# Attention kernel: the first normalization moved from VectorE to ScalarE, and VectorE's loop end moved by half a pair

## The chip, the cores and the metric

The kernel runs on one core of one Trainium2 chip. The metric is the device time of one execution in microseconds; the kernel before takes 2465.89 us (median of three runs, 2464.13 to 2466.8). Five engines work side by side, each with its own list of instructions, and they meet only at semaphores: TensorE (PE in the profile), VectorE (DVE), ScalarE (ACT), GpSimd (POOL) and SyncE (SP), which here issues the DMAs.

## The reference, cut to what matters

One transformer layer over 64 batches of 128 rows and 512 columns, 16 heads of 32 columns:

```python
emb = silu(_sin_emb(timestep)) @ W_ada + b_ada
scale, shift = split(emb[:, None, :], 2, axis=-1)
x = _ln(src) * (1.0 + scale) + shift          # _ln: (x - mean) / sqrt(var + 1e-5)
q, k, v = x @ Wq + bq, x @ Wk + bk, x @ Wv + bv
scores = einsum('bhqd,bhkd->bhqk', q / sqrt(32), k) + attention_bias
probs = softmax(where(src_mask, -inf, scores))
x = x + (einsum('bhqk,bhkd->bhqd', probs, v) @ Wo + bo)
h = _ln(x) * g2 + beta2
ff = _gelu2(h @ W1 + b1) @ W2 + b2            # x * sigmoid(1.702 x)
return x + ff
```

The change touches only the first `_ln`, that of `src`.

## The kernel before, in words

Three parts follow each other: a short setup (the gains and offsets of the layer, the weights split in a high and a low piece), the attention (to about 1110 us of the profile) and the feed-forward part. Products are made from three matmuls each, high times high, high times low and low times high.

The attention works on 32 pairs of batches. A step is half a pair: step (p, 0) attends to batch t = 2p, step (p, 1) to batch t = 2p + 1, and in the same step the engines prepare later batches: step (p, 0) makes the keys and step (p, 1) the queries of pair p + 1, both make values, both turn (transpose) a batch of pair p + 2, and the statistics and the normalization run ahead of that by up to one pair more. The 16 heads of a batch go in four groups. The order on each engine is written out by hand. `run` (L579) unrolls the steps of pairs -2 to 3 and 28 to 32, and puts pairs 4 to 27 in a loop of six iterations of four pairs, eight steps each. VectorE has its own frame, `run_halves` (L897): it cuts a step in `first_half` and `second_half` and places the end of its loop (L904) between the two halves of an even step, (p, 0).

The names that matter below:

- `normalize` (L117) makes xn = (xin - mean) * rstd for one batch, on VectorE, as the last thing of `first_half` of every step: the second batch of pair p + 2 in step (p, 0), the first batch of pair p + 3 in step (p, 1).
- `statistics` and `spread` (L102, L107), in step (p, 0) only, right after it: mean and variance of pair p + 3. They write over `mean`, so `spread` first waits until both batches of pair p + 2 are normalized: `xn_ready` must have reached 2(p + 3). The seven small instructions of the variance are in `variance` (L48); POOL makes rstd of it in `root` (L113).
- `residual` (L122): POOL multiplies xn by the gains and adds the offsets (L127, L129). PE turns the result (L135), ACT copies it as xT_hi (L140), DVE makes xT_lo (L145).
- `second_half` begins with `context` (L68, L70): DVE splits psC, the product of the probabilities and the values (PE L962), into cT_hi and cT_lo, from which PE makes the output projection (psD<-wo, L923 to L925). Then come the reciprocals of the softmax sums (`invert`, L791, a group each), which POOL waits for (L597), and xT_lo.
- `first_half` begins with the four score additions (L780), then `add_bv` (L772, the values), the maxima (L785), `negate_mask` (L796), and `add_residual` (L806, L808), which frees psD[0].
- PE: `project_t` makes keys or queries in four pieces, a = 0 to 3. Piece 0 waits for `add_bv` of the same step, and piece 1 for L806 of the same step.
- ACT: `copy_k` and `copy_q` (L698, L702) copy the four pieces out of psD, `exps` (L713) makes the exponentials of a group, `copy_pT` (L708) copies turned probabilities, `norm.high` is L140.
- SP: `norm.load` (L94) fetches xin of pair p + 4 in step (p, 0), once `xn_ready` has reached 2(p + 3); `load_gains` (L98) stands behind it.

Of the kernel before, what the change touches and what calls it, by code (L numbers as in the profile page):

```python
# [25 lines left out]
ALU = mybir.AluOpType  # L26
# [14 lines left out]
def at_least(eng, sem, count):  # L41

    if isinstance(count, int) and count <= 0:
        return
    eng.wait_ge(sem, count)
# [27 lines left out]
class FirstNorm:  # L73

    def __init__(self, nc, ctx, hold, x, ident, psX):
        sb = lambda name, shape, dt=F32: ctx.enter_context(nc.sbuf_tensor(name, shape, dt))
        sem = lambda name: hold.enter_context(nc.semaphore(name))
        B, _, DM = x.shape
        self.DM, self.CH, self.ident, self.psX = DM, DM // P, ident, psX
        self.rows = x.rearrange("b s n -> s b n")  # L80
        self.xin, self.xn = sb("xin", [P, 2, 2, DM]), sb("xn", [P, 2, DM])
        self.xres, self.adab = sb("xres", [P, 4, 2, DM]), sb("adab", [P, 2, 2 * DM])
        self.st, self.part = sb("st", [P, 2, 6]), sb("part", [P, 4, 2])
        self.mean, self.ve, self.rstd, self.expo = sb("mean", [P, 2]), sb("ve", [P, 2]), sb("rstd", [P, 2]), sb("expo", [P, 2])
        self.xT = [[sb(f"xT{u}_{n}", [P, self.CH, 2 * P], F32R) for n in ("hi", "lo")] for u in range(2)]
        self.x_in = [sem(f"x_in{u}") for u in range(2)]
        self.bn_done, self.part_done, self.var_ready, self.rstd_ready, self.xn_ready = (
            sem("bn_done"), sem("part_done"), sem("var_ready"), sem("rstd_ready"), sem("xn_ready"))
        self.adab_in = [sem(f"adab_in{b}") for b in range(2)]
        self.res_half, self.res_ready = sem("res_half"), sem("res_ready")  # L90
        self.xt_done, self.x_hi, self.x_split = sem("xt_done"), sem("x_hi"), sem("x_split")
        self.w_low = {n: sem(f"w{n}_low") for n in "vkq"}
# [21 lines left out]
        at_least(pool, self.var_ready, q + 1)  # L114
        pool.tensor_tensor(self.rstd[:, :], self.ve[:, :], self.expo[:, :], ALU.pow).then_inc(self.rstd_ready, 1)

    def normalize(self, dve, q, u, b):  # L117
        at_least(dve, self.rstd_ready, q + 1)
        at_least(dve, self.res_half, q * 2 + (b - 1))
        dve.tensor_scalar(self.xn[:, b, :], self.xin[:, u, b, :], self.mean[:, b:b + 1], self.rstd[:, b:b + 1],  # L120
                          ALU.subtract, ALU.mult).then_inc(self.xn_ready, 1)

    def residual(self, pool, q, slot, b):
        out = self.xres[:, slot, b, :]
# [208 lines left out]
def setup_part(nc, block, hold, d, w, norm, ada_rows, bq_s, bk_c, bv_bc, raw_o, wo_in, bo_bc):  # L333
# [6 lines left out]
    with ExitStack() as ctx:  # L340
# [85 lines left out]
        @block.scalar  # L426
        def _(act):
            def high(i):
                act.wait_ge(w_in[i], DMA)
                if names[i] == "v":  # L430
                    act.activation(split_w[i][0][:, :, :], raw[i][:, :, :], ACT.Copy).then_inc(w_hi, 1)
                    return
                for c in range(CH):
                    last = act.activation(in_slots(split_w[i][0], c), by_slot(raw[i], c), ACT.Copy)
                last.then_inc(w_hi, 1)

            act.wait_ge(rest_ok, 1)
            act.activation(emb[:, :], rest[:, :], ACT.Sin).then_inc(sin_ok, 1)
            act.wait_ge(sin_ok, 1)
            act.activation(expm[:, :], emb[:, :], ACT.Exp, scale=-1.0).then_inc(exp_ok, 1)  # L440
            for i in range(3):
                high(i)

# [16 lines left out]
        @block.vector  # L460
        def _(dve):
            count = [0]

            def then(ins):
                count[0] += 1
                ins.then_inc(chain, 1)
                dve.wait_ge(chain, count[0])


            dve.wait_ge(small_in, 3 * DMA)  # L470
            then(dve.tensor_copy(col[:, 0:1], t_int[:, :]))
            then(dve.tensor_scalar(col[:, 1:2], col[:, 0:1], 1.0 / NUM_STEPS, None, ALU.mult))
            then(dve.tensor_copy(q_hi[:, :], col[:, 1:2]))
            then(dve.tensor_tensor(col[:, 2:3], col[:, 1:2], q_hi[:, :].bitcast(F32), ALU.subtract))
            then(dve.scalar_tensor_tensor(out=col[:, 3:4], in0=q_hi[:, :].bitcast(F32), scalar=-NUM_STEPS,
                                          in1=col[:, 0:1], op0=ALU.mult, op1=ALU.add))
            then(dve.scalar_tensor_tensor(out=col[:, 4:5], in0=col[:, 2:3], scalar=-NUM_STEPS,
                                          in1=col[:, 3:4], op0=ALU.mult, op1=ALU.add))
            then(dve.scalar_tensor_tensor(out=col[:, 5:6], in0=col[:, 4:5], scalar=1.0 / NUM_STEPS,
                                          in1=col[:, 1:2], op0=ALU.mult, op1=ALU.add))  # L480
            then(dve.tensor_scalar(col[:, 6:7], col[:, 5:6], RESCALE, None, ALU.mult))
            then(dve.tensor_scalar(angle[:, :], freqs[:, :], col[:, 6:7], None, ALU.mult))

            k, r = turns[:, :], rest[:, :]
            dve.wait_ge(quarter_ok, 5)
            then(dve.tensor_scalar(k, angle[:, :], 1.0 / TWO_PI, quarter[:, 0:1], ALU.mult, ALU.add))
            then(dve.tensor_scalar(k, k, ROUND, None, ALU.add))
            then(dve.tensor_scalar(k, k, ROUND, None, ALU.subtract))
            then(dve.scalar_tensor_tensor(out=r, in0=k, scalar=-PI_A, in1=angle[:, :], op0=ALU.mult, op1=ALU.add))
            then(dve.scalar_tensor_tensor(out=r, in0=k, scalar=-PI_B, in1=r, op0=ALU.mult, op1=ALU.add))  # L490
            then(dve.scalar_tensor_tensor(out=r, in0=k, scalar=-PI_C, in1=r, op0=ALU.mult, op1=ALU.add))
            then(dve.tensor_scalar(r, r, quarter[:, 1:2], None, ALU.add))
            dve.tensor_scalar(r, r, 3.1415925, -3.1415925, ALU.min, ALU.max).then_inc(rest_ok, 1)
            norm.statistics(dve, 0, 0)
            norm.spread(dve, 0)

            dve.wait_ge(exp_ok, 1)
            then(dve.tensor_scalar(expm[:, :], expm[:, :], 1.0, None, ALU.add))
            then(dve.reciprocal(expm[:, :], expm[:, :]))
            dve.tensor_tensor(gate[:, :], emb[:, :], expm[:, :], ALU.mult).then_inc(gate_ok, 1)  # L500
            norm.normalize(dve, 0, 0, 0)
            dve.wait_ge(gate_turned, 1)
            dve.tensor_copy(embT[:, :, :, :], psT[:, :, :].rearrange("p c (a b) -> p a c b", a=2)).then_inc(embT_ok, 1)
            dve.wait_ge(bias_in, 11 * DMA)
            dve.tensor_scalar(bq_s[:, :], bq_raw[:, :], HD ** -0.5, None, ALU.mult)
            low(dve, 0, range(CH))

            dve.wait_ge(ada_done, 1)
            dve.scalar_tensor_tensor(out=ada[:, 0:DM], in0=psA[:, 0, :], scalar=1.0, in1=b_ada[:, 0:DM],
                                     op0=ALU.add, op1=ALU.add).then_inc(ada_ok, 1)  # L510
            dve.wait_ge(ada_done, 2)
            dve.tensor_tensor(ada[:, DM:], psA[:, 1, :], b_ada[:, DM:], ALU.add).then_inc(ada_ok, 1)
            low(dve, 1, range(CH))
            low(dve, 2, range(CH // 2))
# [21 lines left out]
def attention_part(nc, block, hold, d, w, norm, ada_rows, resid, psD, bq_s, bk_c, bv_bc, bo_bc, raw_o, wo_in, second, weights):  # L536
# [7 lines left out]
    with ExitStack() as ctx:  # L544
# [149 lines left out]
        def _(act):  # L694
# [22 lines left out]
            def step(p, u, b, on):  # L717
# [26 lines left out]
                    exps(t, b, 1)  # L744
                if on.proj:
                    copy(*kq, 3)
                if on.turn:
                    norm.high(act, p + 2, u % 2, b)
                if on.attn:
# [18 lines left out]
        def _(dve):  # L768
# [41 lines left out]
            def first_half(p, u, b, on):  # L810
# [22 lines left out]
                else:  # L833
# [15 lines left out]
                    if on.attn:  # L849
                        for g in range(2, G):  # L850
                            highest(t, b, g)
                if on.norm:
                    if b:
                        norm.normalize(dve, p + 3, (u + 3) % 2, 0)
                    else:
                        norm.normalize(dve, p + 2, u % 2, 1)
                if on.stats:
                    norm.statistics(dve, p + 3, (u + 3) % 2)
                if on.attn:
                    invert(t, b, 0)  # L860
                if on.stats:
                    norm.spread(dve, p + 3)

            def second_half(p, u, b, on):
                t = p * 2 + b
                if on.prev:
                    context(t - 1)
                if on.attn:
# [27 lines left out]
            def run_halves():  # L896

                first, last = 4, PAIRS - 5
                for p in range(-2, first):
                    for b in range(2):  # L900
                        first_half(p, p % UNROLL, b, half(p, b, PAIRS))
                        second_half(p, p % UNROLL, b, half(p, b, PAIRS))
                first_half(first, first % UNROLL, 0, steady(0))
                with dve.Fori(0, (last - first + 1) // UNROLL) as i:  # L904
                    for m in range(2 * UNROLL):
                        u, b = divmod(m, 2)
                        second_half(i * UNROLL + (first + u), (first + u) % UNROLL, b, steady(b))
                        u, b = divmod(m + 1, 2)
                        first_half(i * UNROLL + (first + u), (first + u) % UNROLL, b, steady(b))
                for p in range(last + 1, PAIRS + 1):  # L910
                    for b in range(2):
                        if p > last + 1 or b:
                            first_half(p, p % UNROLL, b, half(p, b, PAIRS))
                        second_half(p, p % UNROLL, b, half(p, b, PAIRS))

            run_halves()

# [795 lines left out]
```

## Time and profile before

| | |
|---|---|
| median of three runs | 2465.89 us (2464.13 to 2466.8) |
| the profiled execution, its time | 2472.93 us |
| its span, first to last instruction | 2471.1 us |
| its mean granted TensorE clock | 0.988 |
| PE busy, matmuls | 2363.4 us, 96% |
| DVE busy | 1830.4 us, 74% |
| POOL busy | 1840.8 us, 74% |
| ACT busy | 1323.4 us, 54% |

The page gives busy time over the whole span. The attention and the feed-forward part have different limits, so the busy shares say little about a change in one of them; the timeline of each engine in one pair of steps, the idle time in square brackets with what ended it, and the chain of waits around VectorE's loop end say more. Times in rows are in us from the start of the span.

### The profile page before, as it was taken

How to read it: one execution, taken by the hardware profiler on the slowest of the kernel's cores; microseconds unless marked ns; L12 is line 12 of the kernel's file. 1: busy time of each engine (PE TensorE's matmuls, PEld its weight loads, DVE VectorE, ACT ScalarE, POOL GpSimd, SP SyncE). 2: the span in 40 equal slices, each digit the busy share in tenths (PEclk: the TensorE clock that was granted, in tenths of full speed). 3: DMA queues.
4: the chain of work that ended last, by engine and by line, in shares of the span. 5: the costliest groups of instructions: out<-in, count | busy, mean ns of one | idle time of the engine just before them, and what ended most of it. 6: DMA issues, size and time to landing. Idle time of an engine off the chain costs nothing.

```text
span 2471.1 us, 61234 instructions
## 1 busy us (share of the span) xinstructions
PE 2363.4 (96%) x21010; PEld 2234.2 (90%) x21010; DVE 1830.4 (74%) x2921; ACT 1323.4 (54%) x3663; POOL 1840.8 (74%) x1785
## 2 busy tenths in 40 slices
PE   4999999999999999987999999999989999999998
PEld 3888888888888888867999999999979999999998
DVE  4788888888888888777666666666577676777776
ACT  2566666566666666575555555555543333343332
POOL 3777777777777777778777777777896777767675
PEclk8999999999999999999999999999999999999999
DMA  7344444344434444333343434343465556555563
GB/s 241 109 134 134 139 140 134 110 134 139 139 115 137 135 139 136 102 90 122 147 159 136 161 144 154 141 161 146 159 219 170 185 181 188 184 183 187 170 196 125
DMA packets 288978, 372.26 MB, mean 151 GB/s; under 512 B 28544, under 2 KB 202752, under 8 KB 288768
## 3 DMA queue, kind: packets, MB, share of 16 engines
q1 hardware_dynamic: 288768, 369.57, 46.2%
q8 instruction: 118, 1.93, 0.3%
q14 instruction: 92, 0.75, 0.1%
HBM read 251.81 MB, written 117.70 MB: 150 GB/s over the span
## 4 chain that ended last, share of the span: by engine, by line
PE 85%; DVE 5%; issue 3%; POOL 3%; ACT 1%; DMA 1%; SPq 0%; DVEq 0%; POOLq 0%; ACTq 0%
PE up L1568 14%; PE up L1566 14%; PE up L1567 14%; PE turn L923 5%; PE psD L923 4%; PE psD L924 4%; PE psD L925 4%; PE turn L925 4%; PE turn L924 4%; PE psS L952 4%; PE psC L962 2%; PE psS L938 2%; PE turn L1566 2%; PE turn L1567 2%; PE turn L1568 2%
## 5 line engine op out<-in xcount | busy, mean ns | idle before, releaser
L1566 PE MATMUL up<-T,wc 128*128 128x256 f32 x1792 | 511.2, 285 | 14.7 <-DVE gu L1440 7.0
L1568 PE MATMUL up<-T,wc 128*128 128x256 f32 x1792 | 508.0, 283 | 0.0
L1567 PE MATMUL up<-T,wc 128*128 128x256 f32 x1792 | 505.4, 282 | 0.0
L597 POOL TENSOR_TENSOR s<-s,rinv 128x512 f32<-128x512 f32 x254 | 265.2, 1045 | 234.2 <-DVE rinv L791 231.7
L713 ACT ACTIVATE s<-s,nmx 128x128 f32<-128x128 f32 x1024 | 396.2, 394 | 5.5 <-issue 5.5
L1566 PE MATMUL up<-wc,gs 128*128 128x256 f32 x1280 | 360.2, 281 | 3.2 <-DVE gs L1523 3.2
L657 POOL TENSOR_TENSOR bias<-bias,mneg 128x512 f32<-128x512 f32 x256 | 351.8, 1394 | 13.7 <-DVE mneg L796 13.7
L1567 PE MATMUL up<-wc,gs 128*128 128x256 f32 x1280 | 359.9, 281 | 0.0
L1568 PE MATMUL up<-wc,gs 128*128 128x256 f32 x1280 | 359.8, 281 | 0.0
L1566 PEld LDWEIGHTS up<-T,wc 128*128 128x128 f32 x1792 | 339.3, 189 | 18.5 <-DVE gu L1440 8.4
L1567 PEld LDWEIGHTS up<-T,wc 128*128 128x128 f32 x1792 | 340.7, 190 | 0.0
L1568 PEld LDWEIGHTS up<-T,wc 128*128 128x128 f32 x1792 | 337.2, 188 | 0.0
L1523 DVE TENSOR_TENSOR gs<-gbuf,gs 128x768 fp32r<-128x768 f32 (+1 forms) x128 | 197.0, 1565 | 104.2 <-ACT gs L1399 104.2
L1523 DVE TENSOR_TENSOR gs<-gu,gs 128x768 fp32r<-128x768 f32 x126 | 198.5, 1608 | 81.2 <-ACT gs L1399 81.2
L1566 PEld LDWEIGHTS up<-wc,gs 128*128 128x128 f32 x1280 | 241.9, 189 | 3.8 <-DVE gs L1523 3.8
L1567 PEld LDWEIGHTS up<-wc,gs 128*128 128x128 f32 x1280 | 241.9, 189 | 0.0
L1568 PEld LDWEIGHTS up<-wc,gs 128*128 128x128 f32 x1280 | 241.9, 189 | 0.0
L1399 ACT ACTIVATE gs<-gbuf 128x768 fp32r<-128x768 f32 (+1 forms) x128 | 115.2, 945 | 198.8 <-PE up L1568 189.0
L1399 ACT ACTIVATE gs<-gu 128x768 fp32r<-128x768 f32 x126 | 113.5, 946 | 185.9 <-PE up L1568 176.7
L1246 POOL TENSOR_TENSOR gu<-gu,p5c 128x256 f32<-128x256 f32 x128 | 101.7, 794 | 131.5 <-ACT p5c L1340 110.3
L713 ACT ACTIVATION_READ_ACCUMULATOR s<-s,nmx 128x1 f32 x1024 | 197.8, 193 | 0.0
L785 DVE TENSOR_REDUCE nmx<-s 128x4 f32<-128x512 f32 x256 | 167.3, 674 | 0.1
(209 smaller groups left out, 7043.8 us busy)
## 6 DMA issues: line engine op xcount, KB each, us to landing
bias<-in_bias SPq DMA_DIRECT2D x128, 512.0 KB, 5.4
gated<-gu SPq DMA_DIRECT2D x128, 512.0 KB, 2.6
adab<-ada_rows SPq DMA_DIRECT2D x64, 512.0 KB, 5.5
gbuf<-gated SPq DMA_DIRECT2D x64, 512.0 KB, 3.9
gu<-gated SPq DMA_DIRECT2D x63, 512.0 KB, 3.9
xin<-in_x SPq DMA_DIRECT2D x32, 512.0 KB, 5.1
resid<-rout SPq DMA_DIRECT2D x64, 256.0 KB, 2.2
r<-resid SPq DMA_DIRECT2D x16, 1024.0 KB, 6.0
```

Of the source, the lines that this page charges most:

```text
L597: eng.tensor_tensor(s[:, b, heads, :], s[:, b, heads, :], rinv[:, b, heads].unsqueeze(2).to_broadcast([P, HG, S]), ALU.mult).then_inc(done, 1)
L657: pool.tensor_tensor(bias[:, b, heads, :], bias[:, b, heads, :], mneg[:, b, :].unsqueeze(1).to_broadcast([P, HG, S]), ALU.add).then_inc(bi ...
L713: last = act.activation(s[:, b, h, :], s[:, b, h, :], ACT.Exp, bias=nmx[:, b, h:h + 1], accum_out=sums[:, b, h:h + 1])
L785: dve.tensor_reduce(nmx[:, b, heads], s[:, b, heads, :], mybir.AxisListType.X, ALU.max, negate=True).then_inc(nmax_ready, 1)
L923: pe.matmul(out, sh, mh, start=start, stop=False)
L924: pe.matmul(out, sh, ml, start=False, stop=False)
L925: return pe.matmul(out, sl, mh, start=False, stop=stop)
L1399: act.activation(gs[s % 2][:, 0, ops, :], t[:, ops.start + 1:ops.stop + 1, :], ACT.Copy).then_inc(s_hi, 1)
L1523: dve.tensor_tensor(gs[s % 2][:, 1, ops, :], t[:, ops.start + 1:ops.stop + 1, :], gs[s % 2][:, 0, ops, :].bitcast(F32), ALU.subtract).then ...
L1566: pe.matmul(out_ap, sh, mh, start=start, stop=False)
L1567: pe.matmul(out_ap, sh, ml, start=False, stop=False)
L1568: return pe.matmul(out_ap, sl, mh, start=False, stop=stop)
```

## The change

`normalize` goes from VectorE to ScalarE. There it is one activation, rstd * xin + offset, and a new small instruction on VectorE, `center`, makes offset = -mean * rstd for both batches of a pair. ScalarE normalizes in each step behind the copy of the fourth piece of the keys or queries and ahead of xT_hi; `center` stands at the start of `second_half` of odd steps, (p, 1). `statistics`, `invert` of group 0 and `spread` move from the end of `first_half` to the start of `second_half`, which leaves their place in VectorE's order as it was. The wait in `spread` is unchanged. VectorE's loop end, which stays between the halves, is now in the odd step, behind the maxima of a pair's second batch. In the setup the first batch's normalization goes behind ScalarE's exponential.

```diff
@@ FirstNorm
+        self.offset, self.offset_ready = sb("offset", [P, 2]), sem("offset_ready")
...
-    def normalize(self, dve, q, u, b):
+    def center(self, dve, q):
+
         at_least(dve, self.rstd_ready, q + 1)
-        at_least(dve, self.res_half, q * 2 + (b - 1))
-        dve.tensor_scalar(self.xn[:, b, :], self.xin[:, u, b, :], self.mean[:, b:b + 1], self.rstd[:, b:b + 1],
-                          ALU.subtract, ALU.mult).then_inc(self.xn_ready, 1)
+        dve.scalar_tensor_tensor(out=self.offset[:, :], in0=self.mean[:, :], scalar=-1.0, in1=self.rstd[:, :],
+                                 op0=ALU.mult, op1=ALU.mult).then_inc(self.offset_ready, 1)
+
+    def normalize(self, act, q, u, b):
+        at_least(act, self.offset_ready, q + 1)
+        at_least(act, self.res_half, q * 2 + (b - 1))
+        act.activation(self.xn[:, b, :], self.xin[:, u, b, :], ACT.Identity, scale=self.rstd[:, b:b + 1],
+                       bias=self.offset[:, b:b + 1]).then_inc(self.xn_ready, 1)
@@ setup, scalar
+            norm.normalize(act, 0, 0, 0)
@@ setup, vector
-            norm.normalize(dve, 0, 0, 0)
+            norm.center(dve, 0)
@@ attention, scalar step
                 if on.proj:
                     copy(*kq, 3)
+                if on.norm:
+                    if b:
+                        norm.normalize(act, p + 3, (u + 3) % 2, 0)
+                    else:
+                        norm.normalize(act, p + 2, u % 2, 1)
                 if on.turn:
                     norm.high(act, p + 2, u % 2, b)
@@ attention, vector
-                if on.norm:
-                    if b:
-                        norm.normalize(dve, p + 3, (u + 3) % 2, 0)
-                    else:
-                        norm.normalize(dve, p + 2, u % 2, 1)
+
+            def second_half(p, u, b, on):
+                t = p * 2 + b
+                if on.norm and b:
+                    norm.center(dve, p + 3)
                 if on.stats:
                     norm.statistics(dve, p + 3, (u + 3) % 2)
                 if on.attn:
                     invert(t, b, 0)
                 if on.stats:
                     norm.spread(dve, p + 3)
-
-            def second_half(p, u, b, on):
-                t = p * 2 + b
@@ run_halves
                 first_half(first, first % UNROLL, 0, steady(0))
+                second_half(first, first % UNROLL, 0, steady(0))
+                first_half(first, first % UNROLL, 1, steady(1))
                 with dve.Fori(0, (last - first + 1) // UNROLL) as i:
-                    for m in range(2 * UNROLL):
+                    for m in range(1, 2 * UNROLL + 1):
```

## Rows read from the trace of the kernel before

**Rows 1.** The page, busy us (share of the span) and instructions: TensorE.
```profile
PE 2363.4 (96%) x21010; PEld 2234.2 (90%) x21010; DVE 1830.4 (74%) x2921; ACT 1323.4 (54%) x3663; POOL 1840.8 (74%) x1785
```
**Rows 2.** Timeline of PE, line 938: start us, us, engine line op names xcount.
```profile
205.69 1.06 PE L938 MATMUL psS<-kf,qf 32*128 32x128 f32 x28
...
431.04 1.17 PE L938 MATMUL psS<-kf,qf 32*128 32x128 f32 x32
446.88 1.17 PE L938 MATMUL psS<-kf,qf 32*128 32x128 f32 x32
...
984.80 0.95 PE L938 MATMUL psS<-kf,qf 32*128 32x128 f32 x24
```
**Rows 3.** Chain of waits around VectorE's loop end: start us, us, what.
```profile
462.83 4.89 issue
...
594.04 3.91 issue
```
**Rows 4.** Timeline of PE; brackets: idle before it, and what ended it.
```profile
437.81 0.28 PE L923 MATMUL turn<-xT_hi,wq_hi 128*128 128x256 f32 x1
439.99 0.36 PE L923 MATMUL psD<-xT_hi,wq_hi 128*128 128x256 f32 x1
...
469.49 0.47 PE L923 MATMUL psD<-wo_hi,cT_hi 128*128 128x512 f32 x1 [2.64 <-DVE cT_lo L70]
473.11 0.38 PE L923 MATMUL turn<-xT_hi,wq_hi 128*128 128x256 f32 x1 [0.58 <-DVE v L772]
476.15 0.39 PE L923 MATMUL psD<-xT_hi,wq_hi 128*128 128x256 f32 x1 [0.52 <-DVE rout L806]
```
**Rows 5.** Timeline of DVE in one undisturbed pair.
```profile
428.25 0.16 DVE L53 TENSOR_TENSOR part<-st 128x2 f32<-128x2 f32 x1
...
431.05 0.69 DVE L68 CAST cT_hi<-psC 128x512 fp32r<-128x512 f32 x1
432.38 0.17 DVE L791 RECIPROCAL rinv<-sums 128x4 f32<-128x4 f32 x1
...
441.88 1.56 DVE L120 TENSOR_SCALAR xn<-xin,mean,rstd 128x512 f32<-128x512 f32 x1
...
446.43 0.69 DVE L68 CAST cT_hi<-psC 128x512 fp32r<-128x512 f32 x1 [2.90 <-PE psC L962]
```
**Rows 6.** Timeline of DVE behind the loop end of rows 3.
```profile
469.26 0.17 DVE L791 RECIPROCAL rinv<-sums 128x4 f32<-128x4 f32 x1
...
473.65 1.26 DVE L796 TENSOR_SCALAR mneg<-mask 128x128 f32<-128x128 uint8 x1
```
**Rows 7.** Timeline of POOL at the same time.
```profile
473.54 1.29 POOL L129 TENSOR_TENSOR xres<-xres,adab 128x512 f32<-128x512 f32 x1
```
**Rows 8.** Timeline of ACT in the even step of rows 5.
```profile
426.50 0.46 ACT L698 ACTIVATE kf<-psD,bk_c 128x256 f32<-128x256 f32 x1
426.86 1.08 ACT L708 ACTIVATE pT<-psS 128x512 f32<-128x512 f32 x2
...
430.05 0.46 ACT L698 ACTIVATE kf<-psD,bk_c 128x256 f32<-128x256 f32 x1
431.14 0.60 ACT L140 ACTIVATE xT_hi<-turn 128x512 fp32r<-128x512 f32 x1 [0.64 <-PE turn L135]
```
**Rows 9.** Groups by form, ACT: out<-in shapes xcount, busy us, mean ns of one, idle before.
```profile
L708 ACT ACTIVATE pT<-psS 128x512 f32<-128x512 f32 x256 | 138.5, 595 | 11.8 <-PE psS L952 11.8
L255 ACT ACTIVATE hTf<-turn,be_c,g_c 128x256 f32<-128x256 f32 x120 | 59.1, 562 | 0.0
L1335 ACT ACTIVATE p1c<-up 128x256 f32<-128x256 f32 x128 | 49.0, 383 | 151.3 <-PE up L1568 135.0 <-DVE gu L1435 15.4
```
**Rows 10.** Timeline of DVE in an early step, POOL idle beside it.
```profile
38.28 0.16 DVE L53 TENSOR_TENSOR part<-st 128x2 f32<-128x2 f32 x1
...
39.17 0.69 DVE L145 TENSOR_TENSOR xT_lo<-turn,xT_hi 128x512 fp32r<-128x512 f32 x1
```
**Rows 11.** Timeline of PE, step (0, 1).
```profile
85.61 0.38 PE L923 MATMUL turn<-xT_hi,wq_hi 128*128 128x256 f32 x1 [1.82 <-DVE v L772]
```

More of the change, by code:

```diff
@@ L911, in run_halves @@
                     for b in range(2):
+                        if p > last + 1:
+                            first_half(p, p % UNROLL, b, half(p, b, PAIRS))
                         if p > last + 1 or b:
-                            first_half(p, p % UNROLL, b, half(p, b, PAIRS))
-                        second_half(p, p % UNROLL, b, half(p, b, PAIRS))
+                            second_half(p, p % UNROLL, b, half(p, b, PAIRS))
             run_halves()
```

## The prediction

> **What bounds the kernel now.** I read the page first: PE is busy 96% of the span [rows 1]. Only the attention is touched, so the next view is PE's timeline there. The score matmuls, L938, come once a step; in an undisturbed stretch they stand 15.84 us apart [rows 2], and PE has no idle time that a wait ended. PE sets the pace, and work taken off DVE or put on ACT is worth nothing by itself. From 205.69 to 984.80 us lie 48 steps, the six iterations of the loop [rows 2]: 779.11 us, where 48 x 15.84 = 760.32. So 18.8 us are lost, and the same view between the two ends shows where: five iterations are 3.4 to 4.5 us longer than eight steps, and the first is not. The chain of waits puts that at VectorE's loop end, L904. DVE's sequencer takes the jump back and issues nothing for 4.89 us at worst and 3.91 us at best, five times [rows 3]. The jump stands just ahead of `context`, in an even step in which DVE has no idle time; so cT_lo comes late (2.64 us of PE idle in the worst iteration), then the values (0.58) and then the rout addition L806 (0.52) [rows 4]. These three waits with the reordering around them are the 18.8 us. The chain, the idle time in brackets and PE's timeline agree, so this sum I take as the most that the moved loop end can give.
>
> **The moved loop end.** Five jumps remain, and I leave their price at 3.9 to 4.9 us [rows 3]. In an odd step DVE is through with the maxima at 441.88, where the normalization stood, and then waits for PE until 446.43 [rows 5]. With the normalization gone the cover is 446.43 - 441.88 = 4.55 us, less 0.2 for one reciprocal, and `center`, a small instruction (0.16 to 0.2 like its neighbours, up to some 1.3 if POOL is in its way). At 4.9 plus 0.4 `context` would be up to 0.8 late. What is late next is cT_lo, and the worst jump shows its slack: of its 4.89 us only 2.64 were left as idle time of PE [rows 3, 4], so `context` can be some 2.2 late for nothing. The jump is therefore hidden: -18.8 us, bounds 0 (not hidden at all) and -18.8. The Trainium skill, "Runtime: NRT & Kernel Launch", section "Instruction fetch mechanics", says that a taken branch whose target lies outside the two pages held forces a fetch; this row agrees with it for DVE, and by it the stall goes along with the branch, it only gets another cover.
>
> **The normalization on DVE** is removed 64 times, 1.56 us each [rows 5]; for the reason above that gives PE nothing in steady steps. In the even step it only makes DVE idle earlier. The DMAs that SP issues behind the same semaphore (xin, then the gains) go out some 4 us later in the even step; they are needed a pair later, about 30 us, and SP's next store is not due before the next step: nothing.
>
> **The normalization on ACT** is an activation of 512 columns with two operands from SBUF. With two such operands and 256 columns it takes 562 ns; 256 more columns cost 595 - 383 = 212 ns [rows 9]; together 0.775 us, and 0.80 with a little for the SBUF source, which no row with this form shows (bounds 0.70 and 0.90). In the order of ACT it falls into the idle 0.64 us ahead of xT_hi [rows 8], so that xT_hi is 0 to 0.1 late, with slack behind it. ACT pays nothing in steady steps.
>
> **The wait that this turns on.** `spread` in the even step waits until the second batch of pair p + 2 is normalized. Before, DVE had just done that itself. Now it is done on ACT behind the fourth copy of the keys, and DVE waits there with everything behind `spread`: `context`, two reciprocals for which POOL waits, xT_lo, and the whole next `first_half`. Step by step, in the times of the undisturbed pair:
> - The fourth copy starts at 430.05, and the next activation starts 0.36 later, as at 426.50 and 426.86 [rows 8]: 430.41. It ends at 430.41 + 0.80 = 431.21.
> - `spread` has two more waits to pass: some 0.2 (an estimate with the bounds 0.05 and 0.35, since no row shows this form; the nearest are two instructions with a wait between them, 0.1 to 0.2 apart). L53 starts at 431.42.
> - The seven small instructions take 2.80 us before [rows 5], as two of them stood in POOL's way; POOL is idle at the new place, because its group 0 comes earlier (the reciprocal is no longer behind the normalization) and its next work waits for the next reciprocal. The undisturbed price is 39.17 - 38.28 = 0.89 [rows 10]. `context` starts at 432.31 instead of 431.05 [rows 5], 1.26 late.
> - The reciprocal of group 1, which frees POOL, goes from 432.38 to 433.64. From here the disturbed iteration is the pattern, because there too nothing is waited for behind it: from this reciprocal to PE's first query matmul is 473.11 - 469.26 = 3.85, and to PE's piece 1 is 476.15 - 469.26 = 6.89 [rows 4, 6]. So PE could start piece 0 at 437.49, before its 437.81: nothing lost. But piece 1 can start at 440.53 only, and stood at 439.99 [rows 4]: 0.54 us late.
> - The 6.89 hold because L796 starts 0.11 behind POOL's L129 and lasts until it is through [rows 6, 7]; both follow from the same reciprocal, so they keep this distance.
>
> The Trainium skill, "SBUF — State Buffer", section "Who interferes with whom", says the one of VectorE and GpSimd that issues first holds the shared port for its whole instruction and the other fully blocks, and that ACT never waits. The 1.26 us of L796 agree. By the rule taken alone the change is all gain, as ACT would do undisturbed what DVE did blocked; the row of the wait speaks against it.
>
> All pairs with statistics and an L806 in the odd step pay this, p = 1 to 28: 28 x 0.54 = 15.1 us. The bounds for one pair are 0 (the slack of 1.26 - 0.54 = 0.72 not used up) and 0.54 + 0.3.
>
> **The head.** In steps (-1, 1) and (0, 0) ACT has no gap ahead of xT_hi and PE later waits for `add_bv`, twice, as in step (0, 1) [rows 11]; the activation pushes both by its slot of 0.7: 1.4 us (bounds 0 and 3). The setup is covered by the wait for the weights.
>
> **The sum.** -18.8 + 15.1 + 1.4 = -2.3 us. Against the profiled execution's own 2472.93 this is 2470.6; against the median, 2465.89, it is 2463.6. I take the sum over to the median unscaled, since the pairs lie in a stretch at full clock. About 0.2%, 4.9 us, is what a measurement can tell from no change.
>
> **The rivals.**
> - A, the forecast: jump hidden, 0.54 a pair; 0.40 to 0.68 a pair gives 2459.7 to 2467.5. Chance 0.58.
> - B, the wait in `spread` is covered: the activation ends earlier, or L796 issues just ahead of L129 (it is 0.11 away) and L806 comes up to 1.2 earlier. Then -18.8 + 1.4 = -17.4: 2448.5. For it: 0.72 us of slack, the thin distance. Against it: five disturbed iterations, all alike. Chance 0.21.
> - C, slower: `spread` at its new place meets POOL. If one of its instructions waits for a POOL instruction as before (2.80 instead of 0.89, of which one half is about 0.9), a pair loses 1.4 us: -17.4 + 28 x 1.4 = +22, 2488. It decides above 0.80 a pair, where the sum passes +4.9. Against it: POOL waits for the reciprocal that DVE has not yet made. Chance 0.11.
> - D, the change doesn't do what it says: the jump in the odd step is not covered, for example because it now starts with the bias loads that go out behind L808. Without any cover -2.3 + 18.8 = +16.5: 2482; covered by half, 2473. Chance 0.10.
>
> **The numbers.** Faster by over 0.2%: B whole and some 0.15 of A's lower end, 0.36. Slower: C, most of D, 0.19. Within: 0.45. The time is A's, 2463.6. The range goes from 2447, 1.5 below B, to D with half a cover, 2473, which leaves out C, the worse half of D and the edges of B.
>
> **What would show it.** Right: L938 at 31.68 + 0.54 a pair, no longer iteration among them; PE idle ahead of psD<-xT_hi,wq_hi, ended by rout L806, some 0.5 us in each odd step; DVE idle ahead of L53, ended by ACT's xn; the jump's 4 us inside idle time that PE's psC ends. Wrong: L53 with no ACT wait (B), L55 or L57 at 1 us (C), cT_lo ending PE's idle in the step behind the jump (D).

## The result, and the profile after

The changed kernel takes 2476.75 us (median of 20; 2469.77 to 2479.66) beside 2467.94 for the kernel before on the same chip (20; 2463.08 to 2475.41): a ratio of 1.0027 [1.0017, 1.0036]. By the ratio that is slower by 6.7 us (4.2 to 8.9), where 2.3 us less had been forecast; 2476.75 lies above the range. The medians differ by 8.8, since the executions of both kernels fall in two groups some 8 us apart (of which more below), and more of the changed kernel's fall in the upper one. One execution of the change measured again (r4 below) took 5178.39 us; no profile shows why, the ratio given there leaves it out, and the median of ten does not. The profiled execution took 2478.87 us with a span of 2477.1; the kernel before had 2471.1. So its span is 6.0 longer, and this is what the profiles can explain. The page, as [rows 1]:

```profile
PE 2376.5 (96%) x21010; PEld 2241.7 (90%) x21010; DVE 1695.0 (68%) x2889; ACT 1365.0 (55%) x3727; POOL 1841.1 (74%) x1785
```

DVE lost 135 us of work, ACT took on 42, and PE, which sets the pace, got busier by 13 with the same instructions. The timeline of PE, the score matmuls that open a step (start, duration), as [rows 2]:

```profile
405.73 1.17 PE L951 MATMUL psS<-kf,qf 32*128 32x128 f32 x32
...
438.01 1.17 PE L951 MATMUL psS<-kf,qf 32*128 32x128 f32 x32
```

A pair takes 32.28 where 31.68 stood before. Between the two lies the start 422.09: 16.36 for the odd step, 15.92 for the even one. DVE and ACT in this pair, as [rows 5, 8]:

```profile
405.09 0.81 ACT L127 ACTIVATE xn<-xin,offset,rstd 128x512 f32<-128x512 f32 x1
```
```profile
406.02 0.16 DVE L53 TENSOR_TENSOR part<-st 128x2 f32<-128x2 f32 x1 [4.52 <-ACT xn L127]
...
406.91 0.69 DVE L68 CAST cT_hi<-psC 128x512 fp32r<-128x512 f32 x1
...
408.24 0.17 DVE L804 RECIPROCAL rinv<-sums 128x4 f32<-128x4 f32 x1
...
412.63 1.28 DVE L809 TENSOR_SCALAR mneg<-mask 128x128 f32<-128x128 uint8 x1
...
414.43 0.68 DVE L819 TENSOR_TENSOR rout<-psD,xres 128x512 f32<-128x512 f32 x1
```

PE's two pieces behind the reciprocal at 408.24, and PE's waits from 200 to 1000 us (total, times, longest), as [rows 4]:

```profile
412.53 0.28 PE L936 MATMUL turn<-xT_hi,wq_hi 128*128 128x256 f32 x1
...
415.16 0.39 PE L936 MATMUL psD<-xT_hi,wq_hi 128*128 128x256 f32 x1 [0.17 <-DVE rout L819]
```
```profile
PE psD L936 <- DVE rout L819: 5.9, 24, 0.5
```

This is the wait of the forecast: DVE idle until ACT's xn, then rout late, then PE idle ahead of piece 1. From reciprocal to piece 1 it is 6.92, 6.89 had been taken over from the disturbed iteration [rows 4, 6]. Piece 0 comes on time. The idle time of 0.17 is smaller than the loss of the step, because PE's order around the wait spreads it: the matmuls psS<-ident,s, up to the start of what follows them and so with that idle time, take 3.58 us in this pair and 3.17 in a pair before.

The loop end, in DVE's timeline and in the rows of its sequencer (form, ns, start), as [rows 3]:

```profile
L916 DVEq COMPARE_BRANCH  x1: 63/63/63, 350.9 to 350.9; - x1
L916 DVEq FUSED_REGOPS  x1: 70/70/70, 353.9 to 353.9; - x1
```
```profile
353.97 0.52 DVE L121 SCALAR_TENSOR_TENSOR offset<-mean,rstd 128x2 f32<-128x2 f32 x1 [0.70 <-issue]
354.41 0.17 DVE L804 RECIPROCAL rinv<-sums 128x4 f32<-128x4 f32 x1
357.10 0.69 DVE L68 CAST cT_hi<-psC 128x512 fp32r<-128x512 f32 x1 [2.52 <-PE psC L975]
```

The jump takes 3.0 us of the sequencer (2.8 to 3.1 in the five of this profile; 4.0 to 5.0 by the same rows before), and most of that passes while DVE still works off what had been issued; 0.70 are left as idle time. Behind it DVE waits 2.52 us for PE: the jump is hidden.

### The profile page after: what moved, and what is told of

It is laid out like the page before. It is cut to its first block, busy times and chain, and to the rows that moved or that the text cites. A ratio compares the mean times of both kernels' runs of the same rounds, so it can differ in the third digit from the quotient of the medians.

```text
span 2477.1 us, 61290 instructions
## 1 busy us (share of the span) xinstructions
PE 2376.5 (96%) x21010; PEld 2241.7 (90%) x21010; DVE 1695.0 (68%) x2889; ACT 1365.0 (55%) x3727; POOL 1841.1 (74%) x1785
## 4 chain that ended last, share of the span: by engine, by line
PE 75%; DVE 12%; issue 5%; ACT 5%; POOL 3%; DMA 1%; DVEq 0%; SPq 0%; ACTq 0%; POOLq 0%
PE up L1581 13%; PE up L1579 13%; PE up L1580 13%; PE psD L936 3%; PE turn L936 3%; PE psS L965 3%; PE turn L938 3%; PE turn L937 3%; PE psD L937 3%; PE psD L938 3%; PE turn L1579 2%; PE turn L1581 2%; PE turn L1580 2%; DVE s L793 2%; ACT s L721 2%
```

## The experiments

All of them compute the whole reference. The tables give medians in us. The kernel before, run beside them, had 2467.53 (e1 to e4), 2469.98 (e5 to e8), 2470.34 (r1 to r4) and 2471.38 (s1 to s4). "Even, odd" are the two steps of an undisturbed pair in the profile.

**Each part alone.** E2 is the kernel before with the loop end moved and DVE normalizing as it did; E3 is the changed kernel with the loop end back in the even step.

```diff
 # e2, against the kernel before (e3 the other way round, against the changed one)
+            def second_half(p, u, b, on):
+                t = p * 2 + b
                 if on.norm:
...
+                second_half(first, first % UNROLL, 0, steady(0))
+                first_half(first, first % UNROLL, 1, steady(1))
                 with dve.Fori(0, (last - first + 1) // UNROLL) as i:
-                    for m in range(2 * UNROLL):
+                    for m in range(1, 2 * UNROLL + 1):
```

> The kernel before with only VectorE's loop end moved into the odd step, behind the maxima; normalization stays on VectorE. Theory (the jump is hidden in the idle time that ends with psC): the five iterations with a jump lose nothing or up to 0.5 us each where they lost 3.4 to 4.5, a time 15 to 19 us below the kernel before. Rival (the jump stalls wherever it stands, and the changed kernel only pays for it elsewhere): within 5 us of the kernel before.

> The kernel with the loop end alone once more, since its first measurement had four runs. If the loop end is worth the five stalls and nothing else, the time is 15 to 19 us below the kernel before; the first measurement had 20. Its step of 15.75 us comes again if it belongs to the program, and is 15.84 or 15.92 if it belongs to the execution.

> The changed kernel with VectorE's loop end back in the even step, so the normalization's move alone. Theory (in the even step VectorE now idles some 4.5 us ahead of L53 for ScalarE's normalization, and the jump of 3 to 5 us falls into that): the five jumps cost at most 0.5 us each more, so the time is within 3 us of the changed kernel, and a pair takes 32.27. Rival (only the moved loop end hides the jump): some 17 us above the changed kernel, 24 above the kernel before.

| kernel | median (n) | ratio to before | even, odd | step at an iteration's end |
|---|---|---|---|---|
| before, again (r1) | 2470.22 (10) | 1.0004 [0.9988, 1.0019] | 15.84, 15.84 | 19.5 to 20.1 |
| loop end alone (e2) | 2447.95 (4) | 0.9916 [0.9888, 0.9944] | 15.75, 15.75 | 15.75 |
| the same again (r2) | 2448.16 (6) | 0.9917 [0.9899, 0.9934] | 15.84, 15.84 | 15.84 |
| ACT normalizes, loop end as before (e3) | 2473.47 (10) | 1.0020 [1.0007, 1.0034] | 15.92, 16.35 | 16.37 |
| the change again (r4) | 2471.70 (10) | 1.0012 [0.9995, 1.0029] | 15.92, 16.35 | 16.71 |

> The kernel before, unchanged, as one more profile of it. It tells whether the 15.84 us of an undisturbed step belong to the program or to the execution: if to the program (its addresses), 15.84 again; if to the execution or the chip, another value, such as 15.92 or 15.75, and then the 0.08 us a step are not the change's.

> The changed kernel, unchanged, on the same chip. By the causes found so far: 15.92 in even steps and 16.3 to 16.4 in odd ones if both belong to the program, 3 to 10 us above the kernel before, and 20 to 27 above the loop end alone.

R1 is the kernel before unchanged; the first profile of it had 19.2 to 20.4 in the last column. R4 is the change unchanged: its steps came as expected, its time only 0.12% above the kernel before, with an interval that holds no change. So the 6.7 us rest on the first measurement, and r4 does not contradict them. R2, the timelines of PE over the second jump and of DVE at the first:

```profile
441.38 1.17 PE L941 MATMUL psS<-kf,qf 32*128 32x128 f32 x32
...
473.06 1.17 PE L941 MATMUL psS<-kf,qf 32*128 32x128 f32 x32
```
```profile
342.08 0.57 DVE L120 TENSOR_SCALAR xn<-xin,mean,rstd 128x512 f32<-128x512 f32 x1 [0.92 <-issue]
...
345.89 0.69 DVE L68 CAST cT_hi<-psC 128x512 fp32r<-128x512 f32 x1 [3.15 <-PE psC L965]
```

The loop end alone is worth 17 to 21 us by the ratios of e2, r2 and s3 (s3, below, has one unused semaphore more), which fits the 18.8 of the forecast. That it is more is not shown: the 56 steps behind the head lose 18.3 us in r2 against the first profile of before and 19.9 against r1. It doesn't need the normalization's place on DVE: the normalization behind the jump takes 0.57 here instead of 1.56 (0.55 to 0.86 behind the five jumps; POOL is nearly through by then), and 3.15 us of cover are left. E3 shows the other half: with the normalization on ACT the stalls are gone although the loop end stands where it stood. DVE is idle there for ACT's xn anyway, and the jump, 2.8 to 3.0 us in e3, lies in that idle time. The two parts thus remove the same 18.8 us, and together not twice; what the normalization costs beside that is left over in both e3 and the change.

**The wait in `spread`.** E1 lets `spread` wait for DVE's own offset and moves the wait for ACT's xn to POOL's `root`; e4 leaves the wait and runs ACT's activation ahead of the first copy of the even step.

```diff
 # e1
     def spread(self, dve, q):
-        at_least(dve, self.xn_ready, q * 2)
+        at_least(dve, self.offset_ready, q)
     def root(self, pool, q):
+        at_least(pool, self.xn_ready, q * 2)
 # e4
+                if on.norm and not b:
+                    norm.normalize(act, p + 2, u % 2, 1)
                 if on.proj:
...
-                if on.norm:
-                    if b:
-                        norm.normalize(act, p + 3, (u + 3) % 2, 0)
-                    else:
-                        norm.normalize(act, p + 2, u % 2, 1)
+                if on.norm and b:
+                    norm.normalize(act, p + 3, (u + 3) % 2, 0)
```

> The changed kernel, but spread no longer waits for the normalized batches; POOL's root does, which stands two POOL instructions later, and spread waits only for the center of the pair before. Theory (the wait of spread for ScalarE's normalization costs 0.5 to 0.6 us a pair): PE no longer waits for the rout addition in odd steps, a pair takes 31.7 us again instead of 32.27, and the time falls by some 16 us against the changed kernel, to about 15 to 18 us below the kernel before if the head costs little. Rival (the activation's slot on ScalarE is what costs): a pair stays at 32.2 or more and the time is that of the changed kernel, 5 to 9 us above the kernel before.

> The changed kernel with the even step's normalization on ScalarE moved ahead of the first copy of the keys, into the 4.6 us in which ScalarE waits for PE; the wait in spread stays. Theory: the semaphore is there long before spread asks, a pair takes 31.7 us, PE has no wait for rout, and the time is that of the kernel with the wait moved to root within 3 us, 15 to 18 us below the kernel before. Rival (the wait is not the cause): the time of the changed kernel.

E1 2464.59 (10), 0.9981 [0.9965, 0.9996]; e4 2461.03 (10), 0.9966 [0.9947, 0.9984]. Both have 15.92 in even and odd steps alike and no step of the 56 above 16.1, and PE waits for nothing between 200 and 970 us. E1, the timelines of DVE and of PE (its odd step):

```profile
397.10 0.16 DVE L53 TENSOR_TENSOR part<-st 128x2 f32<-128x2 f32 x1
...
400.88 0.69 DVE L68 CAST cT_hi<-psC 128x512 fp32r<-128x512 f32 x1 [0.90 <-PE psC L976]
```
```profile
401.33 1.17 PE L952 MATMUL psS<-kf,qf 32*128 32x128 f32 x32
...
417.25 1.17 PE L952 MATMUL psS<-kf,qf 32*128 32x128 f32 x32
```

L53 has no wait for ACT, and `context` waits for PE again. Two edits with nothing in common but the wait both take the odd step's excess away, so the wait is its cause. Both expectations of the time missed: 15 to 18 us below the kernel before were expected, and by the ratios it was 4.7 and 8.4. The profiles show where most of that went: the 56 steps take 14.0 and 14.3 us less than before, some 4.5 short of 18.8 for a reason that the next runs look for, and the two steps of the head take 3.3 and 1.1 more. The rest lies behind the attention, where executions differ by more than that.

**The 0.08 us in every step.** Even steps are 15.92 in the changed kernel, where nothing waits, and e1 and e4 keep that. The new tensor `offset` moves every later one up by 32 bytes (xT_hi from 136512 to 136544). E5 is the kernel before with the unused tensor and semaphore, r3 is e2 with them, s3 e2 with the semaphore alone, s4 e2 with the tensor alone. S1 is the changed kernel, and s2 is e4, with the offset in two spare columns of `mean`, so that nothing moves. E6, e7 and e8 are the changed kernel, e1 and e4 with `offset` widened to 64 bytes.

```diff
 # e5, r3 (s3: the semaphore alone, s4: the tensor alone)
+        self.offset, self.offset_ready = sb("offset", [P, 2]), sem("offset_ready")
 # e6, e7, e8
-        self.offset, self.offset_ready = sb("offset", [P, 2]), sem("offset_ready")
+        self.offset, self.offset_ready = sb("offset", [P, 16]), sem("offset_ready")
 # s1, s2
-        self.mean, ... = sb("mean", [P, 2]), ...
+        self.mean, ... = sb("mean", [P, 4]), ...
-        dve.scalar_tensor_tensor(out=self.offset[:, :], in0=self.mean[:, :], ...
+        dve.scalar_tensor_tensor(out=self.mean[:, 2:4], in0=self.mean[:, 0:2], ...
```

> The kernel before with nothing but the unused tensor offset (and its unused semaphore) allocated where the changed kernel allocates it; every tensor behind it, from xT to rout, lies 32 bytes higher in each partition, and no instruction is different otherwise. Theory (the 32 bytes take PE's operands off a 64-byte boundary, and PE is slower by them without any wait): an undisturbed step takes 15.92 us as in the changed kernel, not 15.84, so some 60 steps cost 5 us. Rival (the 0.08 us come from ScalarE or VectorE working beside PE, or from the execution): a step of 15.75 to 15.84 and the time of the kernel before.

> The changed kernel with offset padded to 64 bytes a partition, so that the tensors behind it lie on 64-byte boundaries again; the instructions are the same. Theory (alignment): even steps take 15.84 us or less instead of 15.92, odd ones 16.2 to 16.3 as the wait for rout stays, and the time is 4 to 9 us below the changed kernel, within 3 us of the kernel before. Rival: as the changed kernel.

> The kernel with the wait moved from spread to root, with offset padded to 64 bytes. Theory (loop end, wait and alignment are the three causes and add up): no wait of PE in the loop and steps of 15.75 to 15.84 us, 4 to 9 us below the same kernel without the padding, so 10 to 15 us below the kernel before and some 5 us above the kernel with the loop end alone, which is what the head keeps. Rival (the padding does nothing): 2 to 5 us below the kernel before.

> The kernel with the even step's normalization ahead of the first copy of the keys, with offset padded to 64 bytes. Theory: steps of 15.75 to 15.84 us, no wait in the loop, 12 to 20 us below the kernel before, near the kernel with the loop end alone. Rival (the padding does nothing): 6 to 8 us below the kernel before.

> The loop end alone, with the unused tensor offset in the place where the changed kernel has it. If PE's step depends on the addresses behind it, a step takes 15.92 us and the time is 5 to 10 us above the loop end alone; if it depends on the execution, the two times are equal within 3 us.

> The loop end alone, with one unused semaphore more and no tensor. If the addresses make the step longer: 15.84 us a step and the time of the loop end alone, 20 us below the kernel before. If the semaphore does: 15.92 and 12 below.

> The loop end alone, with the unused tensor and no semaphore. If the addresses make the step longer: 15.92 us a step and 11 to 13 us below the kernel before. If the semaphore does: 15.84 and 20 below.

> The changed kernel with offset in the unused half of the mean tile, so that nothing behind it moves; the instructions are the same. If the addresses make the step longer: even steps 15.84, odd ones 16.25 to 16.3, a time 5 to 9 us below the changed kernel and 0 to 4 below the kernel before, which is where the forecast had it. If the semaphore does: as the changed kernel.

> The kernel with the even step's normalization ahead of the first copy of the keys, with offset in the mean tile. If the addresses make the step longer: 15.84 us in all steps and 5 to 9 us below the shifted one, so 14 to 19 us below the kernel before. If the semaphore does: 15.92 and 8 to 10 below.

| kernel | moved by | median (n) | ratio to before | even, odd |
|---|---|---|---|---|
| e5, before | 32 B | 2474.31 (12) | 1.0019 [1.0006, 1.0032] | 15.92, 15.92 |
| e6, change | 64 B | 2472.30 (12) | 1.0015 [1.0001, 1.0030] | 15.92, 16.37 |
| e7, e1 | 64 B | 2460.28 (11) | 0.9969 [0.9952, 0.9986] | 15.92, 15.92 |
| e8, e4 | 64 B | 2460.79 (12) | 0.9959 [0.9945, 0.9972] | 15.92, 15.92 |
| r3, e2 | 32 B | 2456.98 (6) | 0.9951 [0.9937, 0.9966] | 15.92, 15.92 |
| s3, e2 | 0 | 2451.32 (4) | 0.9931 [0.9906, 0.9957] | 15.84, 15.84 |
| s4, e2 | 32 B | 2450.50 (4) | 0.9920 [0.9897, 0.9943] | 15.92, 15.92 |
| s1, change | 0 | 2473.81 (10) | 1.0002 [0.9990, 1.0015] | 15.84, 16.33 |
| s2, e4 | 0 | 2457.41 (5) | 0.9943 [0.9922, 0.9964] | 15.84, 15.84 |

In the profiles this has no exception: of eleven with the tensor at the new addresses all have 15.92, and of seven without none has it: five have 15.84, e2 has 15.75, and s2 has 15.75 up to 319 us and 15.84 behind it, for which I have no reason. The semaphore does nothing. Where the time goes is seen in the matmuls themselves, with nothing waiting. PE's timeline, first and tenth matmul of the same piece, first r2 (not moved), then r3:

```profile
448.16 0.28 PE L926 MATMUL turn<-xT_hi,wk_hi 128*128 128x256 f32 x1
...
449.19 0.28 PE L926 MATMUL turn<-xT_hi,wk_hi 128*128 128x256 f32 x1
```
```profile
451.54 0.28 PE L927 MATMUL turn<-xT_hi,wk_hi 128*128 128x256 f32 x1
...
452.60 0.28 PE L927 MATMUL turn<-xT_hi,wk_hi 128*128 128x256 f32 x1
```

Nine distances take 1.03 us in r2 and 1.06 in r3: 0.114 and 0.118 each. My reason for it fell: I took it that xT_hi had lost a 64-byte boundary, but in e6 to e8 its address is a multiple of 64 again (136576) and the steps stay at 15.92. PE's timeline narrows it. In a pair without a jump, the products that read xT (values, keys and queries) take 17.51 us in r1, r2 and s3, 17.66 in r3, s4, e5 and e4, and 17.68 in e7 and e8; all other matmuls of the pair take 14.16 to 14.18 in every one of them, though cT, kf, qf, pT and v moved as well. So the excess is in the products with xT, and no 64-byte boundary is the rule; what the rule is, is open.

Addresses are not all that sets this pace. In the feed-forward part wc and gs lie at the same addresses in all these kernels, and yet their matmuls follow each other in 0.117, 0.119 or 0.120 us, one value for an execution from some 1900 us to the end, at full granted clock and with nothing waiting. PE from 2050 to 2350 us (length, busy, matmuls, granted clock, DMA share, GB/s), e2 and then r2, which are the same kernel:

```profile
2050.00:2350.00 300.00, 300.00 (x2503) 1.00 0.59 185
```
```profile
2050.00:2350.00 300.00, 300.00 (x2559) 1.00 0.60 186
```

The change had 0.119 in its first profile and 0.117 in r4. From one value to the next the time behind the attention grows by some 6.5 us, which is most of the distance of the two groups of executions. No run tells what chooses the value.

In the times the effect of the address is at the edge. Sixty steps of 0.08 are 4.8 us. R3 is 8.8 above r2 and e5 0.19% above before, s2's ratio lies 0.0023 below e4's and s1's 0.0010 and 0.0025 below those of the change; but s4 and s3, with four executions each, differ the other way. The rest of the kernel differs from execution to execution by more than this: of the kernel before, some lie around 2464 and some around 2472. So several expectations of the time missed though the steps came: s4 is 21 us below before and not 11 to 13, s1 2.4 above it and not 0 to 4 below, and e7 and e8 lie 9.7 and 9.2 below, where their rivals, the padding doing nothing, had at most 5 and 8.

## Why the prediction was wrong

The profiled executions differ by 6.0 us, and this divides as follows. Up to the first of these steps (64.71 against 64.43) 0.3; the two steps of the head 34.60 against 30.38, that is 4.2; the 56 steps behind them 905.78 against 905.83, that is 0; what follows 1472.0 against 1470.5, that is 1.5.

**The moved loop end: right.** -18.8 us was taken, and r2 shows it: no step from the third to 980 us is longer than 16.10. The estimated cover of 4.55 us less 0.4 was not even needed in full, since the jump cost 2.8 to 3.1 at its new place. It doesn't cost a fixed time, and the place alone doesn't set it: e3 has the loop end at the old place and jumps in 2.8 to 3.0. The long ones, 4.0 to 5.0, are in the three profiles (before, r1, e5) in which DVE normalizes and the loop end stands in the even step; why is open. What the forecast missed is that the normalization on ACT hides the jump by itself (e3). That changes no term of the sum, but it turns the credit round: the loop end needs no normalization on ACT to be worth 18.8.

**The wait in `spread`: right in every link, size nearly right.** The activation was to start 0.63 ahead of the score matmuls (measured 405.09 against 405.73, 0.64), to take 0.80 (0.81), `spread` to start 0.38 behind them (0.29), its seven instructions to take 0.89 (0.89), and piece 1 to be 0.54 late. The odd step is longer than the even one by 0.43 in the change and by 0.49 in s1, where nothing else is added. In s1 24 pairs at 0.49 and four at 0.37 to 0.41 are 13.3 us, where 28 x 0.54 = 15.1 stood. In the change the same sum is 11.6, because its even steps have grown by 0.08 and its odd ones by 0.02 only: the wait takes up a part of the slower matmuls. Rival B, a covered wait, and rival C, `spread` in POOL's way, did not come.

**A late start that I did not have: +2.1 us.** The six steps at an iteration's end are 16.70, 0.35 longer than the other odd ones. It is not the jump itself. The timelines of ACT, DVE and PE in the first of them:

```profile
340.22 0.80 ACT L127 ACTIVATE xn<-xin,offset,rstd 128x512 f32<-128x512 f32 x1
```
```profile
341.50 0.16 DVE L53 TENSOR_TENSOR part<-st 128x2 f32<-128x2 f32 x1 [4.88 <-ACT xn L127]
```
```profile
350.63 0.39 PE L936 MATMUL psD<-xT_hi,wq_hi 128*128 128x256 f32 x1 [0.50 <-DVE rout L819]
```

L53 starts 0.48 behind the end of xn, where it starts 0.12 behind it in the pair shown above. PE is late at 350.63, before the jump at 350.9, and it comes a sixth time, with L53 at 989.05, where no jump back follows. E6, r4 and s1 have the same six. In e3, with the loop end elsewhere, it is 0.12 to 0.14 in all 24 pairs of the loop, and no step is longer. In the pairs ahead of the loop, whose code is unrolled, it is 0.03, and these are the four with the smaller loss. So it goes with where the waiting instruction stands in the loop's code; by what means I can't say. With all this the steps come to -18.8 + 11.6 + 2.1 + 56 x 0.08 = -0.6, and some 0.5 lie in three steps that are 0.14 to 0.20 longer: -0.1, as measured.

**The addresses: +2.8 us in these steps, missing from the sum.** This is the term that the forecast did not have at all. The edit "add a tensor" was costed at nothing, without being named. What it cost is the difference of two kernels that differ in nothing else: the 56 steps take 905.8 us in the change and 903.0 in s1, so without it they would have gained 2.9 us on the kernel before and not nothing. In kernels where PE waits for nothing in these steps it costs the full 56 x 0.08 = 4.5 (r3 takes 4.2 more than r2).

**The head: mechanism right, size wrong.** The two waits for `add_bv` came as forecast (start, duration, idle before), beside 3.44 and 1.82 before:

```profile
73.20 0.58 PE L936 MATMUL turn<-xT_hi,wk_hi 128*128 128x256 f32 x1 [4.34 <-DVE v L785]
...
88.53 0.39 PE L936 MATMUL turn<-xT_hi,wq_hi 128*128 128x256 f32 x1 [2.42 <-DVE v L785]
```

They are 1.5 longer together, for 1.4 forecast. The other 2.7 are TensorE's clock. The table by stretches (busy of PE, PEld, DVE, ACT, POOL, then the granted clock, DMA share, GB/s), of the changed kernel and then of the kernel before:

```profile
70.00:80.00 10.00, 6.80 (x37) 6.80 (x38) 7.02 (x14) 2.48 (x10) 5.29 (x5) 0.66 0.41 108
80.00:90.00 10.00, 7.58 (x70) 6.40 (x69) 6.21 (x19) 6.64 (x28) 6.25 (x7) 0.94 0.35 117
90.00:100.00 10.00, 10.00 (x118) 9.50 (x121) 3.25 (x7) 8.11 (x27) 6.71 (x6) 0.88 0.51 150
```
```profile
70.00:80.00 10.00, 7.98 (x63) 7.81 (x66) 9.53 (x20) 4.41 (x20) 6.26 (x5) 0.83 0.70 207
80.00:90.00 10.00, 8.18 (x82) 7.21 (x75) 7.36 (x15) 6.57 (x28) 8.94 (x9) 1.00 0.39 111
90.00:100.00 10.00, 10.00 (x115) 8.64 (x113) 5.14 (x11) 7.76 (x32) 7.15 (x8) 1.00 0.17 57
```

A granted clock of 0.66 in ten microseconds is 6.8 us at 1.2 GHz instead of 2.4; with the 0.94 and the 0.88 it is 10.4 in all, where the kernel before has 3.4 from its 0.83. Seven microseconds more at half the clock can cost up to 3.5, and 2.7 is what has to be explained. No run was made for it, but the kept profiles settle it, since e2 and r2 are one kernel, with the same two waits (5.3 and 5.2 us). The two steps of the head in e2 and then in r2, columns as above:

```profile
64.33:97.31 32.98, 27.71 (x241) 25.09 (x241) 21.50 (x40) 17.54 (x63) 20.26 (x18) 0.84 0.39 114
```
```profile
63.83:92.64 28.81, 23.57 (x241) 20.96 (x241) 21.86 (x40) 17.27 (x63) 19.99 (x18) 1.00 0.45 130
```

At 0.84 the same work takes 4.2 us more than at full clock. The kernel before has 0.94 and 30.38 us, the change 0.85 and 34.60: e2's 32.98 with the waits 1.5 longer. What the activation's slot has to do with the clock is less clear. In all seven profiles of kernels with this activation in its slot behind the fourth copy the second of the two steps is 17.34 to 17.42, and the head takes 33.7 to 34.7; in six of the eight with DVE normalizing the second step is 15.1, in e2 and s4 16.73, and the head takes 28.8 to 33.0. E4 and e8, with the activation moved forward, have 15.12 and 15.14, but s2 has 16.72. So the slot goes with the longer step each time, and the other kernels have it now and then too. The forecast's bound of 3 for the head, set without the clock, was too low.

**What follows, 1.5 us,** lies in a part that the change doesn't touch, and differs by more than that between executions of one kernel (1472.0 and 1465.5 in the change, 1477.3 and 1461.7 in e2 and r2). I take it for no effect, but that is not shown: 6.7 us by the ratio are some 2 more than the 4.5 that the profiles have up to there.

**The baseline, 2.1 us,** belongs to neither kernel: the forecast's 2463.6 started from a median of three executions, 2465.89, where twenty gave 2467.94.

The forecast's step that failed is therefore its sum, in two terms. The moved addresses were put at nothing and cost 2.8 us, and 1.4 for the head came out as 4.2, because the clock was left out. With the late start of 2.1, the three longer steps, and the wait at 13.3 instead of 15.1, the steps' 15.1 - 18.8 = -3.7 came out as 0. That the forecast of the wait and of the jump came nearly right in size is no luck; that the errors of the wait (1.8 too high) and of the late start (2.1 missing) nearly cancel is. None of the four rivals had the time of a matmul as a mechanism, and the range's upper end, half a jump without cover, was built from a case that did not occur.

The best of all is the loop end alone: 2447.95 and 2448.16, 0.9916 and 0.9917, faster than both kernels.

## What to carry to other kernels

Before two edits are made together, ask whether they remove the same stall: here either of them takes out all five, and the one that costs nothing (the loop end) would have done. Work moved to an idle engine is not free where the engine it left used its own order as the synchronization; the new semaphore puts everything behind it on the old engine's queue at the new engine's pace, and letting the wait stand where its consumer is (e1), or producing earlier (e4), is what gives the time back. A new tensor, even one of 8 bytes a partition, shifts the addresses of those behind it; where matmuls are back to back, compare their distance in the profile before you put a difference down to the edit, and compare it in more than one profile of each kernel, since here one kernel had two distances in two executions.

## What the runs showed of the hardware that I had not expected

- The pace of matmuls with nothing waiting depends on where their SBUF operands lie: 0.114 or 0.118 us for 128x256, 15.84 or 15.92 for a step, by a shift of 32 or 64 bytes. In the feed-forward part it differs between executions of one kernel, 0.117 to 0.120 us (e2 and r2). The Trainium skill, "SBUF — State Buffer", section "Who interferes with whom", says that PE never waits on anyone; these profiles have no wait in them either, but the same instructions take longer.
- A taken jump of DVE's sequencer took 4.0 to 5.0 us in the three profiles with DVE normalizing and the loop end in the even step (before, r1, e5) and 2.8 to 3.1 in the others, in e3 with the loop end in the even step too.
- DVE's first instruction behind a wait for ACT started 0.03 us behind the end of ACT's in unrolled code, 0.13 in the loop, and 0.48 in the last pair of the loop's code (the change, r4, e6, s1).
- An activation of 512 columns with scale and bias from SBUF takes 0.81 us, in all 64 instances 0.80 to 0.81.
- The same tensor_scalar of DVE takes 1.56 us beside POOL [rows 5] and 0.57 where POOL is nearly through (r2).
